# Two transformer blocks over 16 images on one core: a loop body of three images in place of one

## What is computed

```
h = layernorm(x) * (1 + ca) + sa;  x = x + ga * scan_attention(h)      # step a: state-space scan
h = layernorm(x) * (1 + cb) + sb;  x = x + gb * routed_ffn(h)          # step b: 8 experts, top 2
h = layernorm(x) * (1 + ca) + sa;  x = x + ga * delta_rule(h)          # step c: gated delta rule
h = layernorm(x) * (1 + cb) + sb;  x = x + gb * attention_and_moe(h)   # step d: attention, 8 experts
return x
```

## Time and profile before

| what | value |
|---|---|
| median of 3 runs (range) | 2820.95 us (2813.79 to 2822.22) |
| span of the profiled execution | 2813.2 us |
| PE busy | 2441.0 us (87%) |
| DVE busy | 2212.7 us (79%) |
| ACT busy | 1200.1 us (43%) |
| POOL busy | 549.1 us (20%) |
| 13 passes of the loop, from the top of one to the top of the last | 2188.2 us |

### The profile page before, as it was taken

One profiled execution on the slowest core, in us unless ns is written; L12 is line 12 of the kernel. 1 busy time (PEld: TensorE's weight loads), 2 busy tenths in 40 slices (PEclk: granted clock), 3 DMA queues, 4 the chain that ended last, 5 costly groups with the idle time before them and its releaser, 6 DMA issues.

```text
span 2813.2 us, 61085 instructions
## 1 busy us (share of the span) xinstructions
PE 2441.0 (87%) x22584; PEld 1893.0 (67%) x22584; DVE 2212.7 (79%) x5136; ACT 1200.1 (43%) x2697; POOL 549.1 (20%) x497
## 2 busy tenths in 40 slices
PE   3688989888898988989888898988989889898997
PEld 2466768667686766768667586766758667686776
DVE  6677897878879887787878879887887978879742
ACT  3332536344353543436444353543536444253512
POOL 2122221122222022121112222022121112222010
PEclk7789999999999999999999999999999999999998
DMA  4000000000000000000000000000000000000000
GB/s 132 4 2 3 7 4 1 8 3 8 3 7 2 3 8 3 7 3 4 5 3 8 3 7 2 3 8 3 7 3 5 4 3 8 3 7 2 1 6 3
DMA packets 24835, 21.46 MB, mean 8 GB/s; under 512 B 7218, under 2 KB 21571, under 8 KB 24531
## 3 DMA queue, kind: packets, MB, share of 16 engines
q1 hardware_dynamic: 24530, 17.26, 2.2%
HBM read 15.13 MB, written 2.13 MB: 6 GB/s over the span
## 4 chain that ended last, share of the span: by engine, by line
PE 32%; issue 32%; DVE 27%; POOL 4%; ACT 2%; DVEq 0%; POOLq 0%; ACTq 0%
DVE wide L1382 4%; DVE wide L1394 3%; PE banks L891 3%; PE banks L1198 3%; PE banks L1024 3%; PE banks L1188 3%; DVE wide L1402 3%; PE banks L1016 2%; PE banks L1052 2%; DVE inv L1570 2%; PE banks L1005 2%; DVE inv L1566 2%; PE banks L963 1%; PE banks L1065 1%; DVE inv L1557 1%
## 5 line engine op out<-in xcount | busy, mean ns | idle before, releaser
L1519 DVE SCALAR_TENSOR_TENSOR wide<-pad,conv,wide 128x256 f32<-128x256 f32 x864 | 370.0, 496 | 0.0
L561 POOL TENSOR_TENSOR wide<-wide 128x512 f32<-128x512 f32 x128 | 188.3, 1471 | 832.0 <-DVE wide L1402 472.0
L1394 DVE TENSOR_TENSOR_SCAN wide<-wide 128x1024 f32<-128x1024 f32 x128 | 292.9, 2288 | 1.9 <-ACT wide L667 0.3
L667 ACT ACTIVATE wide<-small,a_neg 128x255 f32<-128x255 f32 x512 | 216.0, 496 | 173.9 <-DVE wide L1394 173.0
L1044 PE MATMUL banks<-hideb,identb 128*128 128x512 bf16 x800 | 272.1, 403 | 0.0
L1188 PE MATMUL banks<-inv,up 128*128 128x256 f32 x1024 | 264.5, 387 | 0.0
L1198 PE MATMUL banks<-down,inv 128*128 128x128 f32 x2048 | 256.5, 276 | 0.0
L1198 PEld LDWEIGHTS banks<-down,inv 128*128 128x128 f32 x2048 | 248.7, 192 | 5.0
L796 ACT ACTIVATE inv<-banks,up1b 128x256 f32<-128x256 f32 x512 | 214.0, 480 | 52.0 <-PE banks L1188 51.5
L1024 PEld LDWEIGHTS banks<-inv,mats 64*64 64x64 f32 x5120 | 168.3, 139 | 63.9 <-issue 62.1
L1024 PEld LDWEIGHTS banks<-inv 64*64 64x64 f32 x5120 | 159.5, 135 | 67.4 <-issue 65.3
(11 more groups left out here) (280 smaller groups left out, 4933.4 us busy)
## 6 DMA issues: line engine op xcount, KB each, us to landing
gates_bc<-gate_rows SPq DMA_DIRECT2D x32, 128.0 KB, 2.9
x<-in_x SPq DMA_DIRECT2D x16, 128.0 KB, 2.1
up<-in_W SPq DMA_DIRECT2D x1, 2048.0 KB
out<-xn_y SPq DMA_DIRECT2D x16, 128.0 KB, 2.1
wide<-in_wmod SPq DMA_DIRECT2D x2, 384.0 KB, 5.6
con<-in_con SPq DMA_DIRECT2D x1, 724.0 KB, 4.7
w_k<-in_Wk SPq DMA_DIRECT2D x1, 512.0 KB
w_q<-in_Wq SPq DMA_DIRECT2D x1, 512.0 KB
```

Source lines behind the costliest of these rows:

```text
L561: g.tensor_tensor(ypart[p % 2], r[:, 0:512], r[:, 512:1024], ALU.add).then_inc(a_yp.h, 1)
L667: last = s.activation(decay[st % 2][:, at + 1:at + T], dt[:, c, 1:T], ACT.Exp, scale=a_neg[:, c, st * SG + q:st * SG + q + 1])
L1394: v.tensor_tensor_scan(state[st % 2], decay[st % 2], drive[st % 2], 0.0, ALU.mult, ALU.add).then_inc(a_h.h, 1)
L1519: v.scalar_tensor_tensor(dst, src, w, dst, ALU.mult, ALU.add).then_inc(c_conv.h, 1)
```

## The change

The loop runs over turns of three images. Its body emits the same string of x and y three times, with i = 3 * turn + 1, + 2 and + 3, so that it runs five times in place of fifteen. i stays a register value, and so do the counts of the waits. The steps, their order, the buffers, the part ahead of the loop, the part behind it and SP's loop stay as they were. Line numbers of the changed kernel are higher by 3 in the steps (by 1 at the loop itself).

```
+IMAGES = 3
...
-            with eng.Fori(1, NB) as i:
-                at = {"x": 0, "y": 0}
-                for half in turns:
-                    name, *args = (first if half == "x" else second)[at[half]]
-                    at[half] += 1
-                    steps[name](i if half == "x" else i - 1, *args)
-            assert at == {"x": len(first), "y": len(second)}
+            with eng.Fori(0, (NB - 1) // IMAGES) as turn:
+                for n in range(IMAGES):
+                    i = turn * IMAGES + (1 + n)
+                    at = {"x": 0, "y": 0}
+                    for half in turns:
+                        name, *args = (first if half == "x" else second)[at[half]]
+                        at[half] += 1
+                        steps[name](i if half == "x" else i - 1, *args)
+                    assert at == {"x": len(first), "y": len(second)}
```

## The result

| | before | changed kernel |
|---|---|---|
| median of the first comparison (4 runs each) | 2820.52 us (2813.79 to 2822.22) | 2778.52 us (2776.08 to 2779.92) |
| ratio, 95% interval | | 0.9857 (0.984 to 0.9875) |
| median of a second comparison (16 and 5 runs) | 2815.28 us (2804.92 to 2820.56) | 2779.46 us (2777.11 to 2784.72) |
| ratio, 95% interval | | 0.9882 (0.9863 to 0.9901) |
| span of the profiled execution | 2813.2 us | 2778.1 us |

By the two ratios the changed kernel is 1.2 to 1.4% faster. The medians differ by 42.0 us in the first comparison and by 35.8 us in the second, the two profiled spans by 35.1 us. Forecast were 33.5 us, 2787.5 us, and a range of 2776 to 2808 us.

A forecast was written before the change was run, and what follows sets the result against it. The prediction took the bound as a PE-DVE chain with a stop on both at each jump back. Ten jumps at 3.35 us gave 33.5 us, so 2820.95 - 33.5 = 2787.5 us, range 2776 to 2808 us.

The forecast's parts named there:

- The jump, not the top of the image, holds the stop: PE and DVE idle about 2.5 us at the loop's jump back; rival blaming the image's top, unchanged time: 0.07.
- The way in: Entering the loop without a jump, L1263 starts 0.04 us behind DVE's preceding instruction, against 2.65 us idle per jump.
- The two parts: At each removed jump: PE gains 2.04 us from L997 to L1005, DVE 2.65 us idle ahead of L1263; not additive.
- the join: First L1547 on DVE, waiting for PE's L1016: from L997, 6.49 us mean at jumps, 3.14 us straight.
- More than either stop, because of the clock: Behind most jumps PE's clock is 0.50, L1005's matmuls taking 2.07 us; straight should keep 1.00, making the gain 3.35 us.
- All of it is carried to the next pass: Behind L1547 the 3.35 us a place persists; rival, only part carried, 20.4 or 24.1 us gained: 0.30.
- The price of a jump: L997 to L1547 shortens by 3.35 us at each of ten removed jumps, 33.5 us in all.
- From the span to the median: The median of the runs before was taken as 7.75 us above the profiled span of 2813.2 us.
- ACT and POOL cost nothing: Their jumps show no visible stop, so 0 was taken; at most 10.6 us lost at the four remaining jumps.
- The same instructions are read as before: Instruction reading stays the same, PE's queue bringing 13 packets a pass; only the restart at a jump falls away.
- Register steps: DVE's register rows fall from 137 to 127.7 an image; gain taken as 0, bound 5.6 us over 15 images.
- The price of a compare-and-branch: About 108 ns by the skill, so ten loop branches would give an estimated 1.1 us; unchanged-time rival's chance 0.07.

The follow-up runs named there:

- PE alone: The kernel before, with the loop body of three images on PE only, the other engines keeping fifteen jumps: 2802.29 us against 2817.81 us, ratio 0.9948.
- DVE alone: The kernel before, with the loop body of three images on DVE only: 2817.45 us against 2817.81 us, ratio 1.0009.
- both: The kernel before, with the loop body of three images on PE and DVE, one image on ACT and POOL: 2782.9 us against 2817.81 us, ratio 0.9884.

## Why the prediction was right

- **The jump, not the top of the image, holds the stop.** Right, and now shown from two sides: the stop goes with the jump (four numbers of jumps: 14, 4, 2 and 0), and on DVE it goes with the announcement while the jump stays. The way in the earlier trace rows was a weaker sign than the prediction made it, since there another row (L1534) stands ahead of the statistics than in the loop. In the changed kernel they stand behind the last residual itself, and only the four jumps left show idle time.
- **The two parts lie side by side and meet in the first product on DVE.** Right: PE alone and DVE alone give 15.5 us and nothing, both give 34.9 us. The forecast of the join was 3.14 us straight; it is 3.10.
- **More than either stop, because of the clock.** Right: eight matmuls that nobody reads bring the clock back to 1.00 behind all fourteen jumps and the join from 6.49 to 5.86 us in the mean.
- **All of it is carried to the next pass.** Right: the joins add up to 35.3 us, the spans differ by 35.1, and from the join to the next `c_decay` a pass takes 161.7 us in place of 161.8, so that nothing was taken up behind it.
- **The price of a jump**, 3.35 us, was about right: the traces show 3.39 us a place (6.49 against 3.10), the later comparisons 3.5 to 3.6 us, the first 4.2. It is not the same in every execution: in the profiled run with three images on ACT and POOL alone PE and DVE jump as before, but the mean join is at 6.86 us, and the span is 2822.6 us.
- **From the span to the median**, 7.75 us, was the step that was off. In every run on record the two are 1.8 to 2.0 us apart (the changed kernel's profiled execution took 2779.92 us with a span of 2778.1 us), so the profiled execution of before took about 2815 us, near the medians of the later comparisons (2815.28 to 2817.81 us), and the 2820.95 us of the first three runs were a high draw. From 2815 us the same sum gives 2781.5 us, 2 to 3 us above what was measured. The measured 2778.52 us lies 2.5 us above the low end of the range, and that end rests on 4.16 us a place, the price of the last jump alone: that the range holds it is in part luck.
- **ACT and POOL cost nothing.** Right: three images on them alone change nothing. ACT's branch is 45 ns with the longer body too, and at the jump shown above ACT waits 4.41 us for PE. By the rule that the prediction takes from the Trainium skill ("Runtime: NRT & Kernel Launch", section "Instruction fetch mechanics") ACT has to wait for a fetch there. The trace agrees as to the fetch: in the changed kernel a packet starts on q14 0.9 us behind each of ACT's four taken branches, before behind none. The stop itself lies under the wait for PE and cannot be read.
- **The same instructions are read as before.** Wrong, without a visible cost: a jump makes an engine read part of them anew. PE's queue brings 189 packets in place of 208, with ten jumps fewer. The other queue brings 117 in place of 97: in the runs above three images on DVE alone take 21 packets away, on ACT and POOL alone they add 40.
- **Register steps, taken as 0.** Right for this change, which keeps nearly all of them; too low as a bound for the whole kernel, unless the clock made the difference. Without any the same straight code is 13.3 us faster, over twice the bound of 5.6 us, which had been worked out for one engine and for a fifteenth of its steps.
- **The price of a compare-and-branch** by itself is even less than the 108 ns of the Trainium skill ("Advanced Engine Details and Errata", section "Control Flow Timing"): 45 ns on ACT and POOL, 63 ns on DVE. What decides is the 2.65 us behind it.

## What to carry to other kernels

Look for idle time that no semaphore ended at the top of a loop body; if two engines that hand work to each other stop there at the same moment, the price is read where they next meet, and freeing one of them may give nothing. The way into and out of a loop is a free experiment: the same rows without the jump. Where code can be longer, several images in a body, or all of them with constant counts, remove the price; where it cannot, an announced branch may, engine by engine. On PE the branch's own row shows whether it did, on DVE only the idle time behind it.

## What the runs showed of the hardware

- Behind ten of fourteen jumps, with stops of PE of 1.5 to 2.8 us, its granted clock fell to the lower of its two levels (a mean of 0.50 to 0.63 in the stretch right behind them); behind the other four, with stops of 1.5 to 2.0 us, it stayed at 1.00. With 1.9 us of matmuls in PE's queue ahead of the branch it was 1.00 behind all fourteen.
- A jump back cost DVE 2.65 us of idle time (0.39 announced) and PE a branch of 3.3 to 4.6 us (0.36 to 0.39 announced in the body of three images, 2.4 to 3.6 in the body of one).
- The fetch behind a jump shows as a packet of an instruction queue some 1.0 us after the branch, also on ACT, whose branch row is 45 ns with and without it.
- All of the image's waits on constants in place of registers went with 13.3 us, 0.9 us an image; a part of it may be the clock (0.96 and 0.97 in the two rows above on the thirteen passes).
